# Attention score tiles in pairs of neighbouring PSUM banks, read by one instruction per pair, in a transformer block on one Trainium2 core

## What is computed

```python
def attn(x, qkv_w, qkv_b, fc_w, fc_b):            # x: (4, 512, 128)
    qkv = (einsum('bnd,ed->bne', x, qkv_w) + qkv_b).reshape(b, n, 16, 24)
    q, k, v = split(qkv, 3, axis=-1)
    a = softmax(einsum('bhqd,bhkd->bhqk', q, k) * 8 ** -0.5)
    out = einsum('bhqk,bhkd->bhqd', a, v)
    return einsum('bnd,ed->bne', out, fc_w) + fc_b + x

def ffn(x):
    h = silu(lin(x, w1, s1)) * lin(x, w2, s2)      # 128 -> 512
    h = gelu(lin(h, h1, s1h)); h = gelu(lin(h, h2, s2h))
    return lin(h, w3, s3)                          # 512 -> 128

x = layernorm(x + attn(x)); x = layernorm(x + ffn(x))
```

## Time and profile before

| | |
|---|---|
| median of 3 runs | 326.8 us (326.24 to 327.55) |
| the profiled execution | 328.06 us |
| its span, first to last instruction | 326.2 us |
| mean granted TensorE clock | 0.955 of full speed |
| TensorE busy | 302.8 us, 93% |
| VectorE busy | 247.5 us, 76% |
| ScalarE busy | 235.1 us, 72% |
| GpSimd busy | 148.0 us, 45% |
| line 803, maxima of S tiles, 256 | 161.5 us busy, 682 ns each |
| line 654, exps of T tiles, 256 | 137.9 us busy, 605 ns each |

### The profile page before, as it was taken

How to read it: one execution, slowest core, us unless ns; L and a number is a source line. 1 busy time by engine, 2 the same in 40 slices (tenths; PEclk the granted TensorE clock), 3 DMA queues, 4 the chain that set the end, 5 groups by cost and what they waited for, 6 DMA issues and landing times.

```text
span 326.2 us, 5521 instructions
## 1 busy us (share of the span) xinstructions
PE 302.8 (93%) x1780; PEld 137.9 (42%) x1780; DVE 247.5 (76%) x516; ACT 235.1 (72%) x433; POOL 148.0 (45%) x227
## 2 busy tenths in 40 slices
PE   8665999999998999999999999999999997999991
PEld 7531123222332333423543435335434351489990
DVE  3769799999989998789987688677774800079974
ACT  3553568988767998798679996897699889438340
POOL 6284039911143891119708992261398805320101
PEclk9895799999999999999999999999999999699996
DMA  6444443132211221311040204020100010000011
GB/s 142 171 103 69 68 157 94 29 53 34 44 25 43 40 36 16 52 30 23 1 74 10 44 12 78 0 44 9 34 2 0 1 34 0 4 0 2 0 34 37
DMA packets 17830, 13.44 MB, mean 41 GB/s; under 512 B 2551, under 2 KB 16648, under 8 KB 17800
## 3 DMA queue, kind: packets, MB, share of 16 engines
q1 hardware_dynamic: 17546, 12.85, 19.0%
q10 hardware_dynamic: 254, 0.20, 0.3%
HBM read 5.51 MB, written 1.05 MB: 20 GB/s over the span
## 4 chain that ended last, share of the span: by engine, by line
PE 63%; POOL 11%; DVE 9%; ACT 6%; issue 4%; DMA 3%; SPq 1%; ACTq 1%; POOLq 0%; DVEq 0%
PE bank L445 25%; PE bank L480 14%; PE bank L465 9%; PE bank L456 8%; POOL hT L990 3%; DMA h_nat<-in_L_ffn_h_w_dram 3%; ACT prob L654 2%; DVE negmax L803 2%; PE bank L420 2%; PE bank L503 2%; POOL hT L987 1%; ACT h_nat L729 1%; DVE y L793 1%; PE bank L438 1%; DVE parts L817 1%
## 5 line engine op out<-in xcount | busy, mean ns | idle before, releaser
L803 DVE TENSOR_REDUCE negmax<-bank 128x1 f32<-128x512 f32 x256 | 161.5, 682 | 26.6 <-PE bank L456 26.1
L654 ACT ACTIVATE prob<-bank 128x512 f32<-128x512 f32 x256 | 137.9, 605 | 26.7 <-PE bank L465 26.1
L480 PE MATMUL bank<-prob,v_sb 128*32 128x512 f32 x512 | 75.1, 625 | 2.6 <-ACT prob L654 2.6
L445 PE MATMUL bank<-act,hT 128*128 128x512 f32 (+1 forms) x320 | 71.0, 363 | 0.4 <-POOL act L1013 0.3
L456 PE MATMUL bank<-stack 61*128 61x512 bf16 x256 | 68.4, 395 | 2.9 <-DMA stack<-parts 1.8
L465 PE MATMUL bank<-stack 64*128 64x512 bf16 x256 | 65.6, 388 | 2.2 <-DMA stack<-mT 1.4
L445 PEld LDWEIGHTS bank<-act,hT 128*128 128x128 f32 x320 | 48.3, 190 | 16.6 <-issue 9.7
L456 PEld LDWEIGHTS bank<-stack 61*128 61x128 bf16 x256 | 16.5, 94 | 60.8 <-issue 44.7
L722 ACT ACTIVATE h_nat<-bank,hs_all 128x512 f32<-128x512 f32 (+1 forms) x40 | 22.8, 603 | 24.2 <-PE bank L445 24.2
L465 PEld LDWEIGHTS bank<-stack 64*128 64x128 bf16 x256 | 15.7, 94 | 37.3 <-issue 23.8
L954 POOL TENSOR_TENSOR rstd<-rstd,mhalf 128x4 f32<-128x4 f32 (+1 forms) x10 | 9.7, 970 | 47.9 <-DVE rstd L784 47.8
(11 more groups left out here) (120 smaller groups left out, 347.1 us busy)
## 6 DMA issues: line engine op xcount, KB each, us to landing
stack<-parts SPq DMA_DIRECT2D x124, 48.0 KB
x_in<-in_L_attn_x_dram SPq DMA_DIRECT2D x4, 256.0 KB, 3.0
h_nat<-in_L_ffn_h_w_dram SPq DMA_DIRECT2D x1, 1024.0 KB, 8.5
work<-in_L_ffn_h_w_dram SPq DMA_DIRECT2D x1, 1024.0 KB, 6.1
res<-in_L_attn_x_dram SPq DMA_DIRECT2D x4, 256.0 KB, 2.8
out_dram<-y SPq DMA_DIRECT2D x3, 256.0 KB, 2.3
work<-in_L_ffn_w_w_dram SPq DMA_DIRECT2D x2, 256.0 KB, 3.5
stack<-mT SPq DMA_DIRECT2D x30, 6.0 KB
```

What stands on the lines that cost most here:

```text
L445: mm = nc.tensor.matmul(dst, w, v, start=first and n == 0, stop=last and n == len(pairs) - 1)
L480: last = nc.tensor.matmul(space("P", pfirst)[at:at + VW, :], v_sb[b % 2][:, kt, of:of + VW], prob[:, t % NP, :], start=kt == 0 and slot % ...
L654: nc.scalar.activation(prob[:, n % NP, :], space("T", n)[:, :], ACT.Exp, scale=SCALE).then_inc(emptied("T", n), 1)
L803: nc.vector.tensor_reduce(negmax[:, g % 2, col:col + 1], space("S", n)[:, :], AX.X, ALU.max, negate=True).then_inc(emptied("S", n), 1)
```

## The change

The eight banks become one PSUM tensor, so an instruction can read across a bank boundary. S tiles 2n and 2n + 1 go to two neighbouring banks, and so do T tiles. One VectorE instruction takes the maxima of two S tiles, 2 x 512 in and two numbers a row out, and one ScalarE instruction the exps of two T tiles into two slots of the ring. Both wait until both matmuls are done. The emptying of both banks is counted on the semaphore of the first; the matmuls stay one to a tile. The tables of order are all new, and "s" and "e" in them now stand for a pair. The number of TensorE's S, T, P and feed-forward matmuls is what it was, and so are the arithmetic and the amount of memory.

```diff
 PE_ORDER = """
-x:0 wq:1 q:2 q:3 v:4 wt:5 wt:6 wt:0 x:1 wt:2 wt:3 wt:5 v:1 wf:6 S:0 S:4 S:1 S:6 S:0 S:2 S:4 S:1 S:3 S:6 S:5 S:0 S:2 m:4 S:1 S:3 S:6 S:5 S:4 S:0 S:2
+x:0 wq:1 q:2 q:3 v:4 wt:5 wt:6 wt:0 wt:1 wt:2 wt:3 wf:5 x:6 S:4 S:5 S:0 S:1 S:4 S:5 S:2 S:3 S:0 S:1 v:4 S:5 S:6 S:2 S:3 m:0 S:0 S:1 S:4 S:5 S:2 S:3
...
 DVE_ORDER = """
-wq r mid r lo db mid lo db v*2 wf s*40 r s r s lo s lo s*4 hs s*16 wx s*3 L or s om s*31 v or s om s*4 r s l1 lo l1 s l1 s l1 s r s l1 lo s Xh s Xl
+wq r mid r lo db mid db lo v wf s*5 v s*17 r*2 s lo s lo s hs s*10 wx s*3 L s*2 or s om s*12 v or s om s*2 r l1*2 r l1 lo l1 s lo l1 s Xh s Xl s t s
...
+    JOINED = "ST"
...
-        banks = [bank(f"bank{i}") for i in range(8)]
+        psum = ctx.enter_context(nc.psum_tensor("psum", [P, 8, 512], F32))
+        banks = [psum[:, i, :] for i in range(8)]
...
-        turn, turns = {}, [0] * len(banks)
+        turn, emptyings, count = {}, [(at, 0) for at in range(len(banks))], [0] * len(banks)
         for name, n, where in walk(PE_ORDER):
             for k, at in enumerate(where):
-                turn[name, n, k] = at, turns[at]
-                turns[at] += 1
+                sent = turn[name, n - 1, 0][0] if name in JOINED and n % 2 else at
+                count[sent] += sent == at
+                turn[name, n, k] = at, emptyings[at], (sent, count[sent])
+                emptyings[at] = sent, count[sent]
...
+        def both(name, n):
+
+            at = turn[name, n, 0][0]
+            return psum[:, at:at + 2, :]
...
                 if what == "e":
+                    n *= 2
                     if n >= NP and (n == NP or P_OF[n - NP] > P_OF[n - NP - 1]):
                         act.wait_ge(ps_pv, P_OF[n - NP] + 1)
-                    act.wait_ge(ps_st, n + 1)
-                    nc.scalar.activation(prob[:, n % NP, :], space("T", n)[:, :], ACT.Exp, scale=SCALE).then_inc(emptied("T", n), 1)
+                    act.wait_ge(ps_st, n + 2)
+                    nc.scalar.activation(prob[:, n % NP:n % NP + 2, :], both("T", n), ACT.Exp, scale=SCALE).then_inc(emptied("T", n), 1)
...
                 if what == "s":
+                    n *= 2
                     g, _, _, col = S_TILES[n]
                     if col == 0:
                         wait(dve, m_parts, g - 1)
-                    dve.wait_ge(ps_s, n + 1)
-                    nc.vector.tensor_reduce(negmax[:, g % 2, col:col + 1], space("S", n)[:, :], AX.X,
-                                            ALU.max, negate=True).then_inc(emptied("S", n), 1)
+                    dve.wait_ge(ps_s, n + 2)
+                    half = m_rows(g) // NPART // 2
+                    nc.vector.tensor_reduce(negmax[:, g % 2, 0:2 * half].rearrange("p (e c) -> p e c", e=2)[:, :, col],
+                                            both("S", n), AX.X, ALU.max, negate=True).then_inc(emptied("S", n), 1)
```

More of the change, by code:

```diff
@@ L8 @@
 SP_ORDER = """
-lw lh xin vb xin zq*5 zk zq zk zq*2 zk mrow zk*2 lh zk l3 mrow more xres xin spread mrow spread mrow spread mrow spread mrow xres spread mrow spread
-mrow spread mrow spread mrow*2 spread xres mrow spread*2 out mrow spread mrow xres mrow*2 out*4
+lw lh xin vb zq zk zq*2 zk xin zq*5 mrow zk*4 mrow lh l3 more xres xin spread mrow spread mrow spread mrow*2 spread mrow spread xres spread mrow
+spread mrow spread mrow xres spread mrow spread mrow spread out spread mrow*2 xres mrow*2 out*4
@@ L18 @@
[L18 to L25, removed]
@@ new lines @@
+T:1 P:7 S:2 S:3 T:0 T:1 L:6 S:4 S:5 T:0 T:1 P S:2 S:3 T:0 T:1 S:4 S:5 o:6 S:0 S:1 T:2 T:3 P T:4 T:5 S:2 S:3 m:6 S:0 S:1 T:4 T:5 P S:2 S:3 T:4 T:5 S:0
+S:1 S:4 S:5 T:2 T:3 P S:0 S:1 T:2 T:3 T:4 T:5 S:2 S:3 P S:0 S:1 m:6 T:4 T:5 T:2 T:3 S:0 S:1 T:4 T:5 P S:2 S:3 T:0 T:1 T:4 T:5 P S:0 S:1 T:2 T:3 v:6
+o:4 T:0 T:1 S:2 S:3 P:7 S:5 S:6 T:0 T:1 S:2 S:3 P T:0 T:1 a:4 q:5 T:2 T:3 f:6 q:0 x:1 m:4 T:2 T:3 T:5 T:6 P S:0 S:1 T:2 T:3 P S:4 S:5 S:2 S:3 T:0 T:1
+P T:0 T:1 X:6 T:4 T:5 T:0 T:1 P T:4 T:5 S:2 S:3 A:6 B:0 A:1 B:4 S:2 S:3 A:5 B:0 A:6 B:4 S:2 S:3 P S:0 S:1 S:2 S:3 T:5 T:6 H:4 T:0 T:1 S:5 S:6 P S:2
@@ new lines @@
+S:3 S:0 S:1 T:5 T:6 H S:2 S:3 T:5 T:6 P:7 S:0 S:1 T:5 T:6 S:2 S:3 H*2 S:5 S:6 T:0 T:1 P T:2 T:3 m:4 H:0 T:5 T:6 H T:1 T:2 S:3 S:4 H*2 H:5 S:1 S:2 S:3
+S:4 H*2 m:6 H T:0 T:1 H:2 H S:3 S:4 S:5 S:6 T:0 T:1 H*2 P T:3 T:4 S:5 S:6 S:0 S:1 o:2 P S:5 S:6 P S:0 S:1 T:5 T:6 T:2 T:3 S:0 S:1 T:4 T:5 P T:2 T:3
+S:0 S:1 T:4 T:5 P T:2 T:3 S:0 S:1 T:4 T:5 P T:2 T:3 S:0 S:1 T:4 T:5 H:6 H*2 m:2 T:0 T:1 o:3 T:4 T:5 H S:0 S:1 a:2 q:3 q:4 f:5 T:0 T:1 v:6 T:2 T:3 T:0
+T:1 S:4 S:5 P:7 T:2 T:3 P S:4 S:5 S:0 S:1 P T:2 T:3 H:6 H*2 T:4 T:5 X:2 H T:0 T:1 S:3 S:4 H:5 m:6 H A:2 B:0 A:1 B:6 A:3 B:4 H*2 S:0 S:1 H:2 A:6 B:4
@@ new lines @@
+H:6 A:3 B:4 A:5 B:2 A:0 B:1 A:4 H B:2 H*2 H:3 H*2 T:0 T:1 S:4 S:5 H P S:0 S:1 S:5 S:6 T:2 T:3 P S:0 S:1 P S:4 S:5 m:6 S:0 S:1 S:2 S:3 T:4 T:5 P S:0
+S:1 T:4 T:5 W:6 S:2 S:3 W S:4 S:5 T:0 T:1 P T:2 T:3 T:0 T:1 W T:4 T:5 W P T:2 T:3 T:0 T:1 m:4 Y:5 o:6 P:7 T:2 T:3 T:4 T:5 H:0 H T:1 T:2 P T:3 T:4 T:5
+T:6 H*2 H:1 H T:2 T:3 T:4 T:5 H*2 H:6 H T:2 T:3 T:4 T:5 H*2 H:0 H*3 T:1 T:2 P*4 K:0*4 T:3 T:4 T:5 T:6 P K:0 P K:0*2 o:0 K:1*2 a:1 a:2 H:3 f:4 H*3 H:5
+H*3 H:6 H*2 f:7 X:0 H H:1 H*3 A:2 B:4 A:3 B:5 A:7 B:6 W:0 W X:1 W*2 A:2 B:3 A:4 B:7 Y:1 A:0 B:5 A:2 B:6 A:4 B:3 K:0 H:0724 H*9 H:5631 H*9 H:0724 H*9
@@ L35 @@
+H:5631 H*9 W:0 W*3 K:2 W:7 Y:2 W*3 K:0 Y:4
 """
 ACT_ORDER = """
[L38 to L40 removed]
@@ L56 @@
+gl gh gl gh gl gh gl m da*2 mid db mid db p1 m xr u*4 gh*2 gl gh*2 gl*3 m h0 l0 h0 l0 h0*2 l0*2 p2 m gh*2 gl*2 gh gl gh gl m p1 xr u*4 m gh*2 gl*2 gh
+gl gh gl m h0 l0 h0 l0 h0*2 l0*2 p2 gh*4 gl*4 p1*2 p2*3
 """
@@ L281, in emptied @@
         def emptied(name, n, k=0):
-            return f_ev[turn[name, n, k][0]]
+            return f_ev[turn[name, n, k][2][0]]
         def until_free(eng, name, n, k=0):
-            at, u = turn[name, n, k]
-            wait(eng, f_ev[at], u)
+            _, (sent, times), _ = turn[name, n, k]
+            wait(eng, f_ev[sent], times)
         def until_empty(eng, name, n, k=0):
-            at, u = turn[name, n, k]
-            eng.wait_ge(f_ev[at], u + 1)
+            _, _, (sent, times) = turn[name, n, k]
+            eng.wait_ge(f_ev[sent], times)
+        def both(name, n):
+            at = turn[name, n, 0][0]
+            return psum[:, at:at + 2, :]
         def h_piece(n):
```

37 lines of the change are left out of this document (15 added, 22 removed).

## The result

The changed kernel took **335.2 us** (median) beside 326.6 us for the kernel before, a ratio of 1.023 (95% interval 1.019 to 1.027). Run again, unaltered, on another occasion: 332.8 us, ratio 1.017 (1.013 to 1.020). I had forecast 319.3 with 310 to 332. One of the four executions of the first series took 1193.0 us; it is left out of the ratio, and nothing here shows its cause. The first profiled execution has a span of 333.6 us.

What follows compares the result with a forecast made beforehand. VectorE was taken to set the pace from 40 to 120 us, TensorE from 120 to 262. Terms -3.6 - 0.5 - 5 - 2.4 + 4 = -7.5 us gave a median of 319.3 us, range 310 to 332.

Steps and rivals of the forecast that it cites:

- two tiles side by side: TensorE after 120 us: paired S or T matmuls start together, 0.135 us a tile instead of 0.15, saving 5 us.
- Maxima and exps: VectorE's first stage and ScalarE from 262 to 275 us: wide instructions save starts, 3.6 us and 0.5 us.
- What the pair costs in banks: PSUM banks held until a pair's whole instruction ends: 8 late refills of up to 0.50 us, costing 4 us.
- Fewer changes of work: TensorE's feed-forward matmuls come in 52 visits instead of 64, at 0.20 us a visit, saving 2.4 us.
- Of what else moves ... nothing, +-2 us: Moved input load and transposes, larger gate and up blocks, two added keep-warm steps: no effect, within 2 us.
- Rival 1: Three pairs of banks too coarse, engines wait for each other in turn: slower, 332.3 us with 34 late refills, chance 0.23.

Runs made afterwards that it cites:

- the control: The kernel before with only the bank numbers of its middle part given out again by the old trace's release times: 326.0 us, ratio 0.999.
- the moved sequence: Kernel before with each even tile moved down to its odd partner, single reads, banks given freely by release times: 331.9 us, ratio 1.014 to the kernel before.
- the singles in the same tables: The changed kernel with its new order and bank tables, but each S and T tile read and emptied by its own instruction: 333.5 us, ratio 1.018.
- Late emptying alone: The changed kernel's tables with single instructions starting on their own tile, but both banks of a pair given back by the second: 336.6 us, ratio 1.031.
- the old sequence in pairs: Kernel before with each even tile moved down to its odd partner and banks in pairs: 342.3 us, ratio 1.044 wide; 339.2 us, ratio 1.036 single.
- the kernel with 112 pairs ready at no wait: Kernel before, TensorE's sequence unchanged, new bank numbers, wide reads only where the second tile was ready: 331.8 us, ratio 1.015; all reads single, 332.2 us, 1.013.

## Why the prediction was wrong

**The sign was wrong, and the step that failed is "two tiles side by side", -5 us, with its sentence that the new order only adds to it.** Side by side starts are there: 112 and 118 of 128 pairs start together, 23 and 30 before the change, and the S and T matmuls' busy time fell by 30 us. But in the middle stage I read TensorE's 140.87 of 142 us as work that would end the kernel sooner if there were less of it. The kernel with tiles moved next to each other (331.9 us) has side by side starts for 99 and 103 of 128 pairs and lost about 1% where I had booked a gain of 1.5%. The new sequence with single reads and free banks (332.0) lost 1.5%. That S and T tiles start sooner in twos is no gain where what they wait for is a bank and a reader at the right moment; the held loads point there (24.3 and 28.1 us against 13.2 before), but weakly, since the control has 20.2 without being slower.

Why pairs in the sequence cost that, I can only argue: a reader gets two tiles at once and the second one's bank is held for another instruction's time, 0.6 or 0.5 us, while the other reader gets none. The times for which a bank is held support it for VectorE: from matmul start to the end of its reading an S tile held its bank for 2.31 us in the first stage of the moved sequence, 2.09 before and 2.13 in the control. For T after 120 us it does not (2.18 against 2.26 before).

**Maxima and exps, -3.6 and -0.5 us:** the sizes were right. Durations of 1219 and 1027 ns against 1.21 and 1.04 us worked out, starts 1.13 us apart against 1.12. The figure of the Trainium skill that I had set against it (Perfetto Trace Analysis, Optimizing Scalar/DVE Operations), 125 ns of fixed time for a VectorE operation on PSUM, would have made starts 1.07 us apart by estimate; the trace shows 1.13. Against the singles in the same tables the wide instructions took 6.8 us off VectorE's busy time (239.7 to 232.9) and 7.0 off ScalarE's (234.5 to 227.5), where 9.1 and 7.2 were worked out. The other 7.8 of VectorE's 14.6 us came with the new tables alone. Six exps start after 275 us in the kernel before, where I had read feed-forward alone; at 0.06 us a pair that changes nothing.

**What the pair costs in banks, +4 us:** right in size, and by luck in part, since I took 8 late refills of 0.50 us and the held loads are 61 with 37.6 us in all, instead of 32 with 13.2. Late emptying alone cost 3.0 us. With the wide instructions it adds up to nothing: the change has ratios of 1.017 and 1.023, the singles in the same tables 1.018. What I left out is that neighbouring banks are a price of their own: 7 us in the moved sequence, 1.5 or nothing in the sequence made for them.

**Fewer changes of work, -2.4 us:** the gate and up matmuls' busy time fell from 19.2 to 16.8 us, as much as worked out. The end came later all the same, and no run shows this term by itself.

**"Of what else moves ... nothing, +-2 us":** wrong, in the same way, and this is the term that decided. The sequence costs 5 us, and I took no row for it. Steps of the first feed-forward began at 112.8 us instead of 105.8.

**The rivals.** Rival 1, slower at 332.3, had the sign and nearly the time, with TensorE before banks that VectorE still reads, as the held loads show. Its cause is only partly right: late emptying costs 3 us and is paid back; single reads with banks of their own in the same sequence lose 1.5% all the same. Its tell-tale (VectorE under 90% with several us of waits from 40 us on) was met: 69.71 of 80 us, and 7.2 us of waits there against 1.1. But that tell-tale cannot tell a coarse pair from a bad sequence. The Trainium skill's rule under it (same page and section), that breaking instructions up may let work complete sooner where VectorE and ScalarE aren't saturated but cause bubbles on other engines, fits the old sequence in pairs (339.2 with single reads, 342.3 with wide ones) and not the new one.

**Open:** which property of the new sequence, apart from tiles next to each other, costs its 5 us; the two sequences differ in too many places to undo one by one. The moved sequence also has the first tile of each pair later by up to a few steps, and that was not tried apart from the laying together. For the executions without a profile it is also not known what of the loss is waiting itself and what is the clock that falls behind waits (last section).

## What to carry to other kernels

When engines are coupled through few buffers and fixed orders, a saving on each of them is no saving for all. An engine shown as 99% busy may not be what sets the pace: here the matmuls' busy time fell by 30 us and the end came 7.4 us later. Before pricing wider instructions, price the order and the buffer table that they force, by running just these with the old instructions. And where a table says which buffer comes next, a tile given a buffer that is read late can cost more than the instruction saved: the kernel with 112 pairs ready at no wait lost 1.3 to 1.5%, and its bank numbers alone did it. Where two executions of one kernel differ, lay their profiles side by side by the same instruction: below, that is what tells the clock from the waits.

## What the runs showed of the hardware

An instruction that reads across a PSUM bank boundary pays nothing for it that can be seen: 1219 ns for 2 x 512 columns against 682 for 512, 1.13 us from start to start against twice 0.60.

TensorE's granted clock fell in the middle of the changed kernel. Before the change it was 1.00 from 40 to 276 us. In the first profile of the change it fell to its half (1.2 instead of 2.4 GHz) for 3.4 us each from about 59.5, 148.2, 189.2 and 226.7 us, each time behind waits; here the first:

```profile
57.00:59.30 2.30, 1.29 (x10) 0.38 (x6) 1.96 (x2) 1.73 (x4) 2.22 (x4) 1.00 0.43 68
59.30:62.70 3.40, 3.35 (x16) 0.45 (x14) 1.52 (x2) 2.46 (x5) 3.40 (x5) 0.52 0.20 33
```

In the 2.3 us ahead of the first, TensorE was busy for 1.29. The profile of the second series (span 330.3 us instead of 333.6) has only the last of these, at 224 us, and one of its own at 282. As it is the same kernel, the price can be read by the same instruction in both. Around the fall at 148 us, in the first profile:

```profile
147.93 1.72 PE L483 MATMUL psum<-prob,v_sb 128*32 128x512 f32 x8
...
152.26 0.39 PE L468 MATMUL psum<-stack 64*128 64x512 bf16 x2
```

The same two steps in the second, where the clock was 1.00:

```profile
147.13 1.07 PE L483 MATMUL psum<-prob,v_sb 128*32 128x512 f32 x8
...
149.97 0.39 PE L468 MATMUL psum<-stack 64*128 64x512 bf16 x2
```

The distance between the two profiles grew from 0.80 to 2.29 us. At the falls of 59 and 189 us it grew by 1.2 and 1.3 us, at the second profile's own fall it shrank by 1.1, and from 70 to 147 us it stayed at 0.8. So a fall of 3.4 us cost 1.1 to 1.5 us here, and a wait can cost more than its length.

The clock is not the cause of the whole. Between 40 and 320 us the second profile of the change, the new sequence with free banks and the kernel before are at half clock for 6.8 us each (that of the kernel before from 276.3 to 283.1 us), and their spans are 330.3, 330.0 and 326.2 us: about 4 us of the loss are there with no more time at half clock. Of the other 3.3 us of the first profile, 2.9 are the four steps just read. The four executions of the moved sequence with free banks go the same way, 328.6, 331.1, 332.7 and 336.1 us at mean clocks of 0.965, 0.959, 0.952 and 0.942.
